# A Mamba scan kernel: GpSimd multiplies by C two states at a time, and state 5 gets its drive from ScalarE and TensorE

## The reference

```python
delta = softplus(dt @ dtp_w.T + dtp_b);  A = -exp(A_log)
def step(h, inp):
    u_t, d_t, b_t, c_t = inp
    dA = exp(d_t[:, :, None] * A)
    h = h * dA + (d_t * u_t)[:, :, None] * b_t[:, None, :]
    y = einsum('bdn,bn->bd', h, c_t)
    return (h, y)
_, ys = lax.scan(step, h0, ins)          # 256 steps
y = (ys + xc * Dp) * silu(z);  return y @ out_w.T
# x = x + mamba(x, weights 1) + mamba(flip(x), weights 2)
```

## Time and profile before

| | |
|---|---|
| median of 3 runs | 2616.86 us |
| profiled execution, its own time | 2614.2 us |
| its span | 2612.1 us |
| busy in the span: PE / PEld / DVE / ACT / POOL | 85% / 73% / 86% / 73% / 84% |
| Mamba stage, first to last `gate` | 593.7 to 2087.3 us, 31 intervals |
| chain that ended last, by engine | PE 37%, POOL 19%, DVE 15%, issue 14%, ACT 10% |

### The profile page before, as it was taken

The page is one execution under the profiler, slowest core; times in us unless marked ns, Lnnn a source line. Parts: engine busy times, 40 slices in busy tenths (PEclk is TensorE's granted clock), DMA queues, the critical chain, the costliest instruction groups (busy, mean ns, idle before and its releaser), DMA issues.

```text
span 2612.1 us, 48904 instructions
## 1 busy us (share of the span) xinstructions
PE 2227.8 (85%) x15840; PEld 1908.7 (73%) x15840; DVE 2240.6 (86%) x3430; ACT 1895.3 (73%) x3628; POOL 2198.4 (84%) x1402
## 2 busy tenths in 40 slices
PE   4899999668888898888888888888988768999992
...
GB/s 249 21 48 49 49 50 50 144 94 105 110 103 104 107 106 102 107 107 101 111 101 103 112 100 105 111 107 104 106 107 107 85 161 24 50 49 49 49 49 211
DMA packets 156821, 248.73 MB, mean 95 GB/s; under 512 B 22082, under 2 KB 66018, under 8 KB 155874
## 3 DMA queue, kind: packets, MB, share of 16 engines
...
...
## 4 chain that ended last, share of the span: by engine, by line
PE 37%; POOL 19%; DVE 15%; issue 14%; ACT 10%; DMA 4%; ACTq 0%; DVEq 0%; POOLq 0%; SPq 0%
PE bank L1351 10%; POOL buf L548 8%; DVE buf L917 7%; PE bank L1547 6%; PE bank L1372 6%; PE bank L1422 4%; POOL token_outputs L497 4%; POOL buf L487 4%; PE bank L1522 3%; PE bank L1332 3%; ACT over L1164 3%; DMA buf<-state_rows 2%; ACT scaled L1197 2%; DVE buf L904 2%; POOL buf L535 2%
## 5 line engine op out<-in xcount | busy, mean ns | idle before, releaser
L548 POOL TENSOR_TENSOR buf<-buf 128x1024 f32<-128x1024 f32 x512 | 1199.9, 2374 | 32.4 <-PE bank L1547 27.0
L917 DVE TENSOR_TENSOR_SCAN buf<-over,bank 128x512 f32<-128x512 f32 x832 | 953.8, 1200 | 4.9 <-PE bank L1522 2.7
L1164 ACT ACTIVATE over<-wgu,negA 128x510 f32<-128x510 f32 x832 | 541.5, 709 | 40.3 <-DVE buf L917 28.8
L1547 PE MATMUL bank<-id_sb,buf 128*128 128x128 f32 x4096 | 515.8, 279 | 6.8 <-POOL buf L548 6.8
L1547 PEld LDWEIGHTS bank<-id_sb,buf 128*128 128x128 f32 x4096 | 478.2, 144 | 57.2 <-issue 46.6
L1351 PE MATMUL bank<-parts 128*128 128x256 f32 x3408 | 447.6, 288 | 17.3 <-DVE buf L767 9.2
L1351 PEld LDWEIGHTS bank<-parts 128*128 128x128 f32 x3408 | 420.7, 193 | 36.7 <-issue 36.7
L1197 ACT ACTIVATE scaled<-wd_sb,I 128x256 f32<-128x256 f32 x896 | 377.3, 497 | 22.6 <-PE bank L1522 22.5
L497 POOL DMA_INDIRECT token_outputs<-buf,slot_out x284 | 299.5, 1055 | 87.9 <-issue 84.0
L487 POOL DMA_INDIRECT buf<-token_rows,slot_token x284 | 284.5, 1002 | 95.4 <-issue 82.5
L1522 PE MATMUL bank<-id_sb,scaled 128*128 128x128 f32 x1792 | 256.0, 280 | 88.3 <-ACT scaled L1197 38.2
...
## 6 DMA issues: line engine op xcount, KB each, us to landing
buf<-state_rows SPq DMA_DIRECT2D x608, 256.0 KB, 3.2
token_rows<-buf SPq DMA_DIRECT2D x32, 256.0 KB, 2.3
...
out<-X SPq DMA_DIRECT2D x16, 256.0 KB, 3.6
...
```

Source lines behind the costliest of these rows:

```text
L548: pool.tensor_tensor(hC[:, b, :].rearrange("p (c w) -> p c w", c=C), hs[:, b, :].rearrange("p (c w) -> p c w", c=C), Cs[:, b, :].unsqueeze ...
L917: V.tensor_tensor_scan(hs[:, b, w], dA[:, b, c, :, :].rearrange("p s t -> p (s t)"), source, 0.0, ALU.mult, ALU.add).then_inc(s[f"scan_don ...
L1164: ins = A.activation(dA[:, n % R, c, :, 1:], delta[r][:, c * W:(c + 1) * W].rearrange("p (s t) -> p s t", s=S)[:, :, 1:], ACT.Exp, scale=n ...
L1547: ins = M.matmul(bank[4 + q // 2][:, at:at + P], hC[:, n % R, c * W + q * P:c * W + (q + 1) * P], id_sb[:, :], is_transpose=True, start=Fa ...
```

## The change

- `times_C` takes states n and n + 1 in one instruction of 128 x 2048, after the scan of the second. GpSimd's product of state 3 so comes ahead of the first pair of a unit, and that of state 9 ahead of the third.
- The scan has six places instead of four: the two new ones lie in `wd_sb`, where the expert weights lie later; their load waits for the last product by C.
- State 5 is a turned state. ScalarE scales it, at n = 1.5; the scalings of 6 and 8 move to 3.0 and 4.5. TensorE transposes it into banks 0 and 1 (at the head of n = 4). Its `spread` and VectorE's two products go.
- `SUM_AT` is rewritten in pairs.

```diff
-SUM_AT = {6: (0, 1, 2), 7: (3, 4), 9: (5, 6), 11: (7, 8), 12: (9,), 13: (10,), 15: (11,), 16: (12, 13), 18: (14,
-    15)}
+SUM_AT = {6: (0, 1), 7: (2, 3), 9: (4, 5), 11: (6, 7), 13: (8, 9), 15: (10, 11), 17: (12, 13), 18: (14, 15)}
...
-TURNED_UNITS = (2, 4, 6, 8, 10, 12, 14)
-SCALE_AT = {0.5: (0, 4), 1.5: (0, 6), 3.0: (0, 8), 6.0: (0, 10), 9.0: (0, 12), 12.0: (0, 14), 15.5: (1, 2)}
+TURNED_UNITS = (2, 4, 5, 6, 8, 10, 12, 14)
+TURNED_LOW = (5,)
+SCALE_AT = {0.5: (0, 4), 1.5: (0, 5), 3.0: (0, 6), 4.5: (0, 8), 6.0: (0, 10), 9.0: (0, 12), 12.0: (0, 14), 15.5: (1, 2)}
...
+        R, H_BUFS = 4, 6
+        hs_more = wd_sb[:, 0:2 * CW // D, :].rearrange("p (b k) d -> p b (k d)", b=2)
+        def states(N, count):
+            k = N % H_BUFS
+            return hs[:, k:k + count, :] if k < R else hs_more[:, k - R:k - R + count, :]
...
 def turned_bank(n, c):
+            if n in TURNED_LOW:
+                return bank[c]
...
             sp.wait_ge(s["scaled_done"], turned_before(2 * NP, 0))
+            sp.wait_ge(s["hC_ready"], 2 * NP * NS)
...
-                pool.wait_ge(s["scan_done1"], N + 1)
-                pool.wait_ge(s[f"C_in{b}"], (u * (NS // R) + n // R + 1) * DMA)
-                wait(pool, s["y_done"], N + 1 - R)
-                pool.tensor_tensor(hC[:, b, :].rearrange("p (c w) -> p c w", c=C),
-                                   hs[:, b, :].rearrange("p (c w) -> p c w", c=C),
-                                   Cs[:, b, :].unsqueeze(1).broadcast_to([P, C, W]),
-                                   ALU.mult).then_inc(s["hC_ready"], 1)
+                pool.wait_ge(s["scan_done1"], N + 2)
+                for k in (b, b + 1):
+                    pool.wait_ge(s[f"C_in{k}"], (u * (NS // R) + n // R + 1) * DMA)
+                wait(pool, s["y_done"], N + 2 - R)
+                pool.tensor_tensor(hC[:, b:b + 2, :].rearrange("p b (c w) -> p b c w", c=C),
+                                   states(N, 2).rearrange("p b (c w) -> p b c w", c=C),
+                                   Cs[:, b:b + 2, :].unsqueeze(2).broadcast_to([P, 2, C, W]),
+                                   ALU.mult).then_inc(s["hC_ready"], 2)
...
-                        times_C(p, r, n)
+                        if n % 2:
+                            times_C(p, r, n - 1)
...
-                wait(dve, s["hC_ready"], N + 1 - R)
+                wait(dve, s["hC_ready"], N + 1 - H_BUFS)
...
+                low = n in TURNED_LOW
+                last = max((m for m in TURNED_UNITS if m < n and m not in TURNED_LOW), default=TURNED_UNITS[-1] - NS)
+                if not low:
+                    wait(pe, s["scan_done1"], u * NS + last + 1)
                 for c in range(C):
-                    wait(pe, s["mul_done"], 2 * (vector_before(u, n) - 1 + c))
+                    if low:
+                        wait(pe, s[f"scan_done{c}"], u * NS + n - 1)
+                    else:
+                        wait(pe, s["mul_done"], 2 * (vector_before(u, n) - 1 + c))
```

More of the change, by code:

```diff
@@ L214, in macaron_kernel @@
         te = sb("te", [1, TILES], I32)
-        R = 4
+        R, H_BUFS = 4, 6
         CW = C * W
@@ L273, in macaron_kernel @@
         hs = carve(0, R * CW).rearrange("p (b w) -> p b w", b=R)
+        hs_more = wd_sb[:, 0:2 * CW // D, :].rearrange("p (b k) d -> p b (k d)", b=2)
+        assert H_BUFS == R + 2 and 2 * CW // D <= Y_BUFS * G * 2
+        def states(N, count):
+            k = N % H_BUFS
+            return hs[:, k:k + count, :] if k < R else hs_more[:, k - R:k - R + count, :]
         hC = carve(R * CW, R * CW).rearrange("p (b w) -> p b w", b=R)
@@ L903, in scan @@
                             w = slice(c * W + q * L, c * W + (q + 1) * L)
-                            ins = V.tensor_tensor_scan(hs[:, b, w], bank[c][:, q * L:(q + 1) * L],
+                            ins = V.tensor_tensor_scan(states(N, 1)[:, 0, w], bank[c][:, q * L:(q + 1) * L],
                                                        prod[:, turn % 2, w], 0.0, ALU.mult, ALU.add)
@@ L916, in scan @@
                         source = bank[c]
-                    V.tensor_tensor_scan(hs[:, b, w], dA[:, b, c, :, :].rearrange("p s t -> p (s t)"),
+                    V.tensor_tensor_scan(states(N, 1)[:, 0, w], dA[:, b, c, :, :].rearrange("p s t -> p (s t)"),
                                          source, 0.0, ALU.mult, ALU.add).then_inc(s[f"scan_done{c}"], 1)
@@ L1516, in turn_back @@
                 pe.wait_ge(s["scaled_done"], turned_before(u, n) + 1)
-                last = max((m for m in TURNED_UNITS if m < n), default=TURNED_UNITS[-1] - NS)
-                wait(pe, s["scan_done1"], u * NS + last + 1)
+                low = n in TURNED_LOW
+                last = max((m for m in TURNED_UNITS if m < n and m not in TURNED_LOW), default=TURNED_UNITS[-1] - NS)
+                if not low:
+                    wait(pe, s["scan_done1"], u * NS + last + 1)
                 for c in range(C):
-                    wait(pe, s["mul_done"], 2 * (vector_before(u, n) - 1 + c))
+                    if low:
+                        wait(pe, s[f"scan_done{c}"], u * NS + n - 1)
+                    else:
+                        wait(pe, s["mul_done"], 2 * (vector_before(u, n) - 1 + c))
                     for q in range(G):
```

## The result

The changed kernel takes 2720.26 us (median of 4 runs, 2707.91 to 2741.9), the kernel before 2616.11 beside it: 1.0407 times as long, interval [1.0328, 1.0486] (ratios here and below are worked out over the runs and differ a little from the quotient of two medians). Slower was forecast, but the time lies 42 us above the forecast and above the range's upper end, 2704. The profiled execution took 2707.9 us; its span is 2706.0.

A forecast was written before the change was run, and what follows sets the result against it. Bound: a ring of VectorE's part, then TensorE's part, of each unit. Per pair +3.50 - 0.58 + 0.50 + 0.55 = +3.97 us, times 15.5 is +61.5: 2675.7 profiled, 2678 as median; range 2640 to 2704.

The forecast's parts named there:

- The ring: Mamba stage: VectorE from gate to scan 12, then TensorE from state 13's spread to the next gate, sets each unit's time.
- the four parts: VectorE's and TensorE's parts of both kinds of unit, 30.03, 29.04, 18.73 and 18.59 us: 96.39 a pair before the change.
- Sums, +1.75 a unit: TensorE's part before the gate holds eight states' sums instead of six: +1.75 us a unit, +3.50 a pair.
- State 5, -0.58 and +0.50: VectorE's part: at most 0.58 us gained ahead of `split_lo` with r = 1, 0.50 lost at scan 9 with r = 0.
- The wait of 1.7 at `split_lo`: VectorE with r = 0: its wait for ScalarE's `split_hi` grows from 0.43 to 1.7 us, so nothing is gained there.
- Pairs, 4.51 us: GpSimd's product by C for two states takes 4.51 us; eight pairs save 1.3 us a unit, off the ring.
- GpSimd's lateness, +0.55 a pair: GpSimd's product for state 15 comes 1.3 us late, delaying scan 15 and TensorE's part: +0.55 us a pair, bounds 0 and 2.6.
- The upper bound: With the small terms at their bounds, up to some 5.5 us a pair of units, the forecast reaches 2702 us.
- the bound for state 5: Behind `split_hi` with r = 0: the most that ScalarE's extra scaling could cost, all of its 1.69 us.
- The clock: Rival: TensorE's work thins out in a unit's first half, half clock there, VectorE waits for state 13's spread: 2701 us, chance 0.10.
- the forecast's own case: Main case: the ring's terms add 3.97 us a pair of units, 2678 us, from 2662 to 2702; chance 0.74.

The follow-up runs named there:

- f1: The kernel before with only state 5 turned, plus zero-weight matmuls filling TensorE's waits: 2630.51 us, 1.0064 of before.
- f2: The changed kernel with the states' sums asked for earlier, leaving six states in TensorE's part: 2648.23 us, 1.0136 of before.
- k2: The changed kernel with earlier sums and zero-weight matmuls in TensorE's waits, `split_lo` in its old place: 2625.24 us, 1.0044 of before.
- e1: The kernel before with the new `SUM_AT` alone, single products by C, state 5 on VectorE: 2668.58 us, 1.0208 of before.
- h2: The changed kernel with zero-weight matmuls in TensorE's waits, eight of them ahead of the step's projection: 2699.17 us, 1.0325 of before.
- e5: The changed kernel without its state 5, so pairs, six scan places and new sums remain: 2672.23 us, 1.0223 of before.
- g1: The changed kernel with earlier sums, `split_lo` after the scan of state 6, and zero-weight matmuls in TensorE's waits: 2629.66 us, 1.0053 of before.
- e2: The kernel before with state 5 turned and nothing else changed: 2657.8 us, 1.0173 of before.
- g4: The same kernel as g1 but without state 5 turned, VectorE making its products again: 2627.5 us, 1.0051 of before.

## Why the prediction was right about the sign and wrong about the size

- **The ring: right.** Gate, VectorE, spread for state 13, TensorE, gate. All 94 us of the profiled difference lie between the gates, and the four parts account for other kernels too: over 15.5 pairs those of f1, f2 and k2 give 20, 32 and 13 us more than before; measured were 16, 34 and 11 (medians).
- **Sums, +1.75 a unit: right.** Alone they cost 54 us, and TensorE's part grew by 1.7 to 2.1 us in most units of e1.
- **State 5, -0.58 and +0.50: the sizes came out, one of them by luck.** VectorE's part measured 28.39 and 30.54 in the shorter pattern (forecast 28.46 and 30.53); with the clock held it is 28.5 and 30.9 in f1, 28.3 and 30.5 or 31.2 in h2. But without state 5 it is 28.35 and 29.87 in most units of e5. So the gain with r = 1 is not state 5's: the wait of 0.60 us at 1659.64 went with the new sums alone (e1), and with r = 0 state 5 costs 0.67. The reason that was forecast holds: `split_hi` fixes where VectorE goes on. The wait of 1.7 at `split_lo` with r = 0 was 1.47. With r = 1 it was 1.02, forecast as well, without a number. In g1, where `split_lo` no longer waits, the wait stands at ScalarE's next result.
- **Pairs, 4.51 us: right** (4.555 measured), and worth nothing, since GpSimd is not on the ring (e5 against e1: +4 us).
- **GpSimd's lateness, +0.55 a pair: this step failed.** TensorE's part was forecast at 20.4 us, "without a wait"; it is 21.65. How late GpSimd is was forecast well: product 15 ends 38.25 us after the gate with r = 0 (1710.96 + 2.38 - 1675.09; forecast 37.9). What waits for it was not. The sum did not have the wait for the step product at all, which costs 0.68 us in each unit, and for product 15 it took 0.55 a pair where each unit pays 0.60. Both together are 2.5 a pair by the two parts of TensorE, 1.9 more than forecast, some 30 us over 15.5 pairs; the 2675.7 forecast for a profiled execution become some 2705, and it took 2707.9. GpSimd may go on only when TensorE has summed (the wait of 2.63 us at 1642.87); with the sums asked for earlier both waits are gone (f2). The sums that it waits for there are the ones at the half clock, but the clock is not the cause: held, it leaves TensorE's part at 21.4 and 21.65 (h2). State 5 is needed too: without it (e5) the part is 20.4 and 20.7 in more than half of the units.
- **The upper bound: too low by the prediction's own terms.** Its 5.5 a pair holds the 2.6 of GpSimd's lateness and none of the 1.69 that it gives as the bound for state 5. With both the sum is 3.50 - 0.58 + 1.69 + 2.6 = 7.2 a pair, 112 us, and the case alone reaches 2729, not 2702.
- **The clock: a rival at 0.10, and in fact part of the forecast's own case.** It was priced as one or the other (2701 instead of 2678), but came on top: the longer pattern costs 3.7 us a pair (not 4.7, as one expectation has it), and held 15 of 31 units in one profiled execution (2731.09 us) and two in another (2707.91). That it is also why the median lies 12 us above the profiled execution fits, but is not shown: the other runs have no trace. Fillers take it away (h2, 2699). The mechanism named, TensorE's work thinning out in the first half of a unit, holds; the place is another, the waits for ScalarE at the projection and the turns and not the spread for state 13. The Trainium skill, "TensorE: Matmul & The Clock Gate", section "A second HAM failure mode: psum-queue depth-cycling", describes a kernel in which frequent short idles of TensorE between groups of matmuls make its clock swing between its two levels. The runs here agree: with such waits filled the granted clock rose from 0.946 to 0.967 (e2 to f1) and from 0.944 to 0.961 (the changed kernel to h2), and the time fell by 27 and 22 us.

By the ratios of the mends, the changed kernel's 1.043 (some 112 us of 2613.43; 107 by the medians) divides so: with six states in TensorE's part again and GpSimd on time (f2), 1.0136 is left, some 77 us less; with the clock held too (k2) 1.0044 is left, 24 us less; the last 11 us are VectorE's part with r = 0, 0.7 us a unit. There `split_lo` starts 10.98 us after the gate as it did before, and the loss comes behind it, where one row names a wait of 0.17 us for TensorE's spread and the others none. That the rest is ScalarE's lateness is likely, since it has one scaling more there, but not shown. Nor did it go without state 5: g4, with `split_lo` moved, was no faster than g1. In another order of mends the shares may differ. Why the half clock comes at one of two places, and why one run starts with the longer pattern and another doesn't, stays open.
